# A residual chain of four conditioned layers on one core: V of four pairs in one burst of small tiles, a shorter setup, and a new order of each turn

## The chip, the cores and the metric

The kernel runs on one core of a Trainium2 chip. The time is device microseconds of one execution; the median of three executions of the kernel before is 199.01 us (198.2 to 202.66). In the profiles PE is TensorE's matmul, PEld its weight load, DVE VectorE, ACT ScalarE, POOL GpSimd, and SP the engine that here only issues transfers.

## The reference

The input x has 64 batches of 64 tokens of 512 features. Four layers follow each other, each a residual, and all are linear:

```
x = x + x Wb^T + scale0[e] * ((x Wt^T) A0[e]^T B0[e]^T) Wp^T     (e: one of 4)
x = x + x W1^T + scale1[f] * (x A1[f]^T) B1[f]^T                 (f: one of 8)
x = x + mix over the 64 token rows by w2[g]                      (g: one of 8)
x = x + mix over the 64 token rows by w3[h]                      (h: one of 200)
```

The last two work on the token axis, the first two on the feature axis, so they commute. The kernel makes one 512x512 matrix g01 of the two dense parts (with the identities), low-rank tables u and V (V has 16 rows per adapter, 64 + 128 in all) and, for each batch, one 64x64 token matrix p. Then out = (p x) g01 + ((p x) u) V.

## The kernel before, in words

Two batches make a pair (128 rows); four pairs make a turn; there are 8 turns. Turn 0 and turn 7 are written out, turns 1 to 6 are a hardware loop. No scheduler sets an order: each engine runs its own list as it is written, and semaphores hold the lists together.

PE's work of a turn, in the names of the code and of the profile:
- **reduce** (out z_ps): z = y u, for the two pairs of a half; 16 matmuls of 128 rows by 32 columns with 64 tokens. Float32 operands, which the profile lists as two instructions for each matmul (x32).
- **mix** (out y_ps): y = p x, in 64x64 tiles, four of them in different quarters of the array; 32 matmuls for two pairs, x64 in the profile.
- **token_mix** (out p_ps): the p of the next turn, 8 matmuls of 64x64, x16.
- **apply** (out o_ps): 12 matmuls of 128x128 by 512 columns for one pair, from yy (y split in a rounded high part and the rest, type fp32r) and g01 (split the same way); one instruction each. Behind them, in the kernel before, 2 matmuls of the same size that add z V, again with a high and a low part of V.

Around it: DVE copies y out of PSUM (`copy_y`, 2 of 4 per half), ACT makes the high part (`high_y`), DVE the low (`low_y`). ACT and DVE add and split z (`z_half`, `sum_z`, `low_z`). ACT copies o out of PSUM (`copy_out`) and doubles V (`double_v`). DVE prepares the operands of token_mix two turns ahead: `add_w3` (one instruction) and `place_w2` (eight small copies by register addresses). PE waits for both in `token_ready`, ahead of the reduce of the turn before that p is used in. POOL selects u (`place_u`) and gathers w3 for a later turn by four indirect DMAs. SP issues the loads of x, the stores, and for each pair four transfers of 16 rows out of the table of V (`fetch_v`).

The setup computes g01, u and V from the weights: transposes, products and splits, with PE at their head; `g01_step(k)` is 12 matmuls, `up_k` are the tables of u for pairs of adapters.

## Time and profile before

| | |
|---|---|
| median of 3 executions | 199.01 us |
| the profiled execution | 200.97 us |
| its span, first to last instruction | 199.1 us |
| PE busy | 177.4 us, 89% |
| DVE, ACT, POOL busy | 96.8, 94.2, 71.7 us |
| granted TensorE clock | full in all 40 slices (2.4 GHz) |

PE is the engine to follow: where it is idle, the trace names what ended the wait. The start of a z_ps burst marks a half turn, so the distance of every second z_ps start is the length of a turn. The time of a burst is best read from its start to the start of the next one, since the ends of matmuls are modelled and overlap the next.

### The profile page before, as it was taken

To read this page: it belongs to the slowest core of one execution; us is meant where nothing else is said; L and a number is where in the kernel's file an instruction comes from. 1 tells how busy PE (TensorE), PEld (TensorE's weight loads), DVE (VectorE), ACT (ScalarE), POOL (GpSimd) and SP (SyncE) were. 2 spreads that over 40 slices of the span, in tenths; PEclk is the share of its full clock that TensorE was granted. 3 is DMA by queue.
4 is the path that set the end of the run, shared out by engine and by line. 5 is a ranking of instruction groups with operands and counts; after the bars stand their busy time and mean duration, and the time that the engine had idled before them with its cause. 6 is when DMAs were issued, how large, how long until landed. Compare 5 with 4: busy or idle time off the path is not lost.

```text
span 199.1 us, 7261 instructions
## 1 busy us (share of the span) xinstructions
PE 177.4 (89%) x2304; PEld 140.1 (70%) x2304; DVE 96.8 (49%) x232; ACT 94.2 (47%) x183; POOL 71.7 (36%) x184
## 2 busy tenths in 40 slices
PE   6599898696889699999898989898898989999992
PEld 6377574575668487878686867777686868787781
DVE  1288588629653651746074527524650646154210
ACT  2365742126336645455463636354544545564521
POOL 2525787030653056306521741373056303113000
PEclk9999999999999999999999999999999999999999
DMA  3999412222372846375555737482847375443412
GB/s 80 394 357 289 155 46 87 53 66 72 84 262 71 266 151 198 87 245 164 179 168 173 248 84 229 119 259 78 256 121 229 99 232 169 151 162 82 180 72 89
DMA packets 19081, 32.39 MB, mean 163 GB/s; under 512 B 5878, under 2 KB 5878, under 8 KB 19062
## 3 DMA queue, kind: packets, MB, share of 16 engines
q1 hardware_dynamic: 17744, 31.11, 50.0%
q0 software_dynamic: 1024, 1.05, 1.8%
q8 instruction: 8, 0.13, 0.3%
q14 instruction: 11, 0.09, 0.1%
q10 hardware_dynamic: 294, 0.01, 0.1%
HBM read 22.98 MB, written 9.18 MB: 162 GB/s over the span
## 4 chain that ended last, share of the span: by engine, by line
PE 59%; issue 11%; DVE 9%; ACT 9%; DVEq 6%; DMA 2%; another core or an unknown queue 1%; POOL 0%; SPq 0%; ACTq 0%
PE o_ps L733 35%; PE y_ps L733 8%; PE z_ps L733 5%; DVE y_all L619 4%; PE spare_ps L733 4%; PE p_ps L733 3%; ACT yy L444 3%; DVEq L667 3%; DVEq L657 2%; DMA w_sb<-in_L_cond_W_dram 2%; DVE w_sel L667 2%; ACT z L477 1%; ACT v_sel L458 1%; PE y_ps L745 1%
## 5 line engine op out<-in xcount | busy, mean ns | idle before, releaser
L733 PE MATMUL o_ps<-g,yy 128*128 128x512 f32 x384 | 95.2, 396 | 0.0
L733 PEld LDWEIGHTS o_ps<-g,yy 128*128 128x128 f32 x384 | 70.8, 188 | 16.2
L340 POOL COPY u_sel<-u_tab 128x64 f32 x128 | 28.0, 242 | 89.8 <-PE z_ps L733 70.1
L330 POOL DMA_INDIRECT w_all<-in_L_cond_weights_dram,w_rows x32 | 31.7, 990 | 12.8 <-issue 9.7
L465 ACT ACTIVATE o_sb<-o_ps 128x512 f32<-128x512 f32 x32 | 19.2, 599 | 33.8 <-PE o_ps L733 32.4
L444 ACT ACTIVATE yy<-y_all 128x512 fp32r<-128x512 f32 x32 | 19.6, 635 | 25.4 <-DVE y_all L619 21.5
L633 DVE TENSOR_TENSOR z_sum<-z_ps,z_half 64x128 f32<-64x128 f32 x16 | 4.5, 282 | 50.4 <-ACT z_half L472 50.4
L626 DVE TENSOR_TENSOR yy<-y_all,yy 128x512 fp32r<-128x512 f32 x32 | 20.7, 690 | 2.9 <-ACT yy L444 1.9
L619 DVE COPY y_all<-y_ps 128x512 f32<-128x512 f32 x32 | 20.6, 686 | 0.5
L733 PE MATMUL o_ps<-v_sel,z 128*128 128x512 f32 x64 | 20.1, 394 | 0.0
L733 PE MATMUL z_ps<-y_all,u_sel 128*32 128x64 f32 x512 | 11.6, 222 | 9.4 <-DVE w_sel L667 5.1
L733 PEld LDWEIGHTS z_ps<-y_all,u_sel 128*32 128x32 f32 x512 | 8.4, 109 | 16.1 <-issue 16.1
L667 DVE COPY w_sel<-w2T 64x64 f32 x64 | 14.6, 229 | 9.7 <-issue 5.0
L733 PE MATMUL y_ps<-p_now,x_raw 64*64 64x64 f32 x1024 | 18.9, 221 | 0.3 <-issue 0.3
L458 ACT ACTIVATE v_sel<-v_sel 64x512 fp32r<-64x512 f32 x32 | 18.5, 624 | 0.4
L733 PEld LDWEIGHTS y_ps<-p_now,x_raw 64*64 64x64 f32 x1024 | 16.6, 134 | 2.1 <-issue 0.8
L641 DVE TENSOR_TENSOR z<-z_sum,z 32x128 fp32r<-32x128 f32 x32 | 9.2, 287 | 12.4 <-ACT z L477 11.9
L733 PEld LDWEIGHTS o_ps<-v_sel,z 128*128 128x128 f32 x64 | 12.0, 188 | 2.5
L477 ACT ACTIVATE z<-z_sum 32x128 fp32r<-32x128 f32 x32 | 9.9, 311 | 6.9 <-DVE z_sum L633 6.5
L472 ACT ACTIVATE z_half<-z_ps 64x128 f32<-64x128 f32 x16 | 4.4, 275 | 6.6 <-PE z_ps L733 6.4
L450 ACT ACTIVATE p_now<-p_ps 128x256 f32<-128x256 f32 x8 | 3.1, 386 | 7.5 <-PE p_ps L733 5.2
L733 PE MATMUL p_ps<-w_now,w_sel 64*64 64x64 f32 x128 | 5.2, 220 | 1.1 <-issue 1.1
(124 smaller groups left out, 139.8 us busy)
## 6 DMA issues: line engine op xcount, KB each, us to landing
x_raw<-in_x_dram SPq DMA_DIRECT2D x16, 512.0 KB
v_sel<-v_table SPq DMA_DIRECT2D x128, 64.0 KB, 2.1
out_dram<-o_sb SPq DMA_DIRECT2D x14, 512.0 KB, 3.1
w_sb<-in_L_cond_W_dram SPq DMA_DIRECT2D x4, 256.0 KB, 4.8
wb_sb<-in_L_cond_W_base_dram SPq DMA_DIRECT2D x4, 256.0 KB, 6.3
wp_sb<-in_L_cond_Wp_dram SPq DMA_DIRECT2D x2, 512.0 KB, 6.8
wt_sb<-in_L_cond_Wt_dram SPq DMA_DIRECT2D x1, 1024.0 KB
out_dram<-o_sb SPq DMA_DIRECT2D x4, 256.0 KB, 2.8
```

The lines of the kernel that those rows point to most:

```text
L330: pool.indirect_dma_start(out=w3_all[:, j, :], out_offset=None, in_=w3_flat, in_offset=bass.IndirectOffsetOnAxis(ap=w3_rows[:, j:j + 1], a ...
L340: nc.gpsimd.tensor_copy(u_sel[u % 2][:, :, b, RANK * part:RANK * part + RANK], u_tab[:, :, bass.ds(e, 1), :].rearrange("p k a r -> p k (a r)")
L444: nc.scalar.activation(yy[u][:, :, 0, :], y_all[u % 2][:, :, :], ACT.Copy).then_inc(yh_set, 1)
L458: nc.scalar.activation(v_sel[u][ZR:, 0, :], v_sel[u][0:ZR, 0, :].bitcast(F32), ACT.Copy).then_inc(v_twice, 1)
L465: nc.scalar.activation(o_sb[:, u, :], o_ps[u % 2][:, :], ACT.Copy).then_inc(o_set, 1)
L477: nc.scalar.activation(z[rows, :, toks], z_sum[rows, :, :], ACT.Copy).then_inc(zh_set, 1)
L619: nc.vector.tensor_copy(y_all[u % 2][:, :, :].rearrange("p k (b t) -> p b k t", b=2), y_of(u)).then_inc(yf_set, 1)
L626: nc.vector.tensor_tensor(yy[u][:, :, 1, :], y_all[u % 2][:, :, :], yy[u][:, :, 0, :].bitcast(F32), ALU.subtract).then_inc(yl_set, 1)
L633: nc.vector.tensor_tensor(z_sum[:, :, :], z_of(slice(0, ZR)), z_half[:, :, :], ALU.add).then_inc(z_summed, 1)
L641: nc.vector.tensor_tensor(z[ZR + ZR // 2 * b:ZR + ZR // 2 * (b + 1), :, toks], z_sum[rows, :, :], z[rows, :, toks].bitcast(F32), ALU.subtr ...
L667: nc.vector.tensor_copy(w2_sel[rows, u, :], w2T[rows, bass.ds(g, 1), :].rearrange("p a c -> p (a c)")).then_inc(w2_placed, 1)
L733: return nc.tensor.matmul(dst, lhsT, rhs, start=start, stop=stop)
```

## The change

1. **V in one burst.** z and V stay plain float32. z holds 32 rows for each pair, in four groups of partitions; `close` issues for the four pairs of the turn 8 matmuls of 32 rows by 64 columns with 512 columns to stream (16 instructions). Each of the eight has its own 32x64 part of the array, and each pair its own PSUM bank: o_ps has four banks now. `sum_z`, `low_z`, `z_half`, `double_v` and the split of V are gone; `copy_z` on ACT copies z.
2. **The order of a turn on PE.** reduce(0), token_mix, apply 0, mix(1), apply 1, reduce(1), apply 2, close, mix(0) of the next turn, apply 3. close opens the sum of pair 3 and closes those of pairs 0 to 2, so these are copied out behind it: 0 and 2 by ACT, 1 by DVE. Pair 3 is copied by DVE when apply 3 is done (`copy_last`).
3. **V is fetched by POOL**, with two indirect DMAs of 128 rows a turn in place of 16 transfers on SP. SP alternates loads and stores.
4. **DVE's order.** place_w2 for two turns ahead moves ahead of the copies; add_w3 moves to the end, behind copy_last.
5. **Setup.** v0 and u0T are computed in plain float32, as 4 + 4 matmuls in the two column halves, where there were 12 + 12 fp32r matmuls and the splits of wt, wpT, b0 and a0T. Four matmuls of g01_step(0) start before the low parts exist. token_mix(0) and mix(0) go ahead of g01 steps 2 and 3, and `copy_y` of turn 0 ahead of the low parts of g01. The ids and scales are loaded by SP and spread over 128 partitions, with `find_row_shift` and `find_v_rows` on DVE.

The core of the diff:

```diff
-            def apply(i, u):
-                n = u % 2
-                wait(pe, o_set, QUAD * i + u - 1)
-                pe.wait_ge(yl_set, QUAD * i + u + 1)
...
-                pe.wait_ge(zl_set, 2 * (2 * i + u // 2 + 1))
-                pe.wait_ge(v_twice, QUAD * i + u + 1)
-
-                mm(o_ps[n][:, :], z[:, n, :], v_sel[u][:, 0, :], False, False)
-                mm(o_ps[n][:, :], z[:, n, :], v_sel[u][:, 1, :], False, True).then_inc(o_done, 1)
+            def close():
+
+                for u in range(QUAD):
+                    opens = u == QUAD - 1
+                    for b in range(2):
+                        rows, to = z_rows(u, b), slice(SEQ * b, SEQ * b + SEQ)
+                        mm(o_ps[u][to, :], z[rows, u // 2, :], v_sel[rows, u // 2, :],
+                           opens, not opens).then_inc(v_done, 1)
...
+            def turn(i, first=False, last=False):
+                reduce_ready(i, 0)
+                if not first and not last:
                     token_ready(i + 1)
...
+                reduce(0)
+                if not first and not last:
+                    token_mix(i + 1)
+                apply(i, 0, lambda: mix_ready(i, 1), first)
+                mix(1)
+                apply(i, 1)
+                reduce_ready(i, 1)
...
+                reduce(1)
...
+                apply(i, 2, v_ready)
+                close()
+                if not last:
+                    mix(0)
+                apply(i, 3, behind_v=True)
```

```diff
+            def copy_last(i):
+                dve.wait_ge(o_done, QUAD * (i + 1))
+
+                wait(dve, o_out[1], 16 * i)
+                nc.vector.tensor_copy(o_sb[:, QUAD - 1, :], o_ps[QUAD - 1][:, :]).then_inc(o_set_dve, 1)
+
+            def turn(i, ahead=True, more=True):
+                pass_y(i, 1)
+                if ahead:
+                    place_w2(i + 2)
+                copy_out(i, 1)
                 if more:
...
+                    pass_y(i + 1, 0)
+                    copy_last(i)
+                if ahead:
                     add_w3(i + 2)
```

```diff
+            def fetch_v(i):
+
+                wait(pool, v_done, 2 * QUAD * i)
+                for h in range(2):
+                    pool.indirect_dma_start(
+                        out=v_sel[:, h, :], out_offset=None, in_=v_table,
+                        in_offset=bass.IndirectOffsetOnAxis(ap=v_rows[:, h, i:i + 1], axis=0)
+                    ).then_inc(v_in, 16)
```

```diff
             for s in range(KC):
-                pe.wait_ge(setup_dve, DVE_DONE[f"wpT_{s}"])
-                for a, b in ((0, 0), (0, 1), (1, 0)):
-                    last = mm(bank_of("v0")[0:R0, :], b0_by[:, a, s, :, :].rearrange("p e r -> p (e r)"),
-                              wpT[:, b, s, :], s == 0 and a == b == 0, s == KC - 1 and a == 1)
+                mm(bank_of("u0T")[0:R0, :], b0_now[:, s, :, :].rearrange("p e r -> p (e r)"), wpT[:, s, :],
+                   s == 0, s == KC - 1)
+                last = mm(bank_of("u0T")[R0:, :], a0T[:, s, :], wt_sb[:, s, :], s == 0, s == KC - 1)
...
-            product(bank_of("u0T")[0:R0, :], lambda a, k: a0T[:, a, k, :],
-                    lambda b, k: wt[:, b, k, :]).then_inc(setup_ps, 1)
```

PE, the first turn of the kernel before, from its first reduce to the second pair's V (names without buffer numbers; a row's `waits` are the semaphores that its engine waits for ahead of it):

```order
L733 MATMUL z_ps<-y_all,u_sel 32x64 [waits x_in1,u_placed,p_set,yf_set,setup_dve]
L733 MATMUL z_ps<-y_all,u_sel 32x64 x15
L733 MATMUL y_ps<-p_now,x_raw 64x64 x32
L733 MATMUL o_ps<-g,yy 128x512 [waits yl_set]
L733 MATMUL o_ps<-g,yy 128x512 x11
L733 MATMUL o_ps<-v_sel,z 128x512 [waits v_twice,zl_set]
L733 MATMUL o_ps<-v_sel,z 128x512
L733 MATMUL p_ps<-w_now,w_sel 64x64 [waits p_set,w3_plus,w2_placed]
L733 MATMUL p_ps<-w_now,w_sel 64x64 x7
```

PE, the second half of the same turn in the changed kernel:

```order
L726 MATMUL z_ps<-y_all,u_sel 32x64 [waits w2_placed,w3_plus,z_set,p_set,u_placed,yf_set]
L726 MATMUL z_ps<-y_all,u_sel 32x64 x15
L726 MATMUL p_ps<-w_now,w_sel 64x64 x8
L726 MATMUL o_ps<-g,yy 128x512 [waits yl_set]
L726 MATMUL o_ps<-g,yy 128x512 x10
L726 MATMUL o_ps<-g,yy 128x512 [waits x_in0,p_set,v_in,z_set]
L726 MATMUL o_ps<-v_sel,z 64x512 x8
L726 MATMUL y_ps<-p_now,x_raw 64x64 x32
L726 MATMUL o_ps<-g,yy 128x512 [waits yl_set]
L726 MATMUL o_ps<-g,yy 128x512 x11
```

The two V matmuls behind each pair's twelve have become eight narrow ones, once a turn, ahead of the next mix and of pair 3's twelve.

DVE, the end of the loop's turn in the kernel before, from the last low part of y to the copies of place_w2:

```order
L626 TENSOR_TENSOR yy<-y_all,yy 128x4x128 [waits o_done,yh_set] x2
L650 REGISTER_ALU
L35 ISA [waits w3_in2]
L653 ISA [waits p_done]
L653 TENSOR_TENSOR w_now<-w_all,ident 128x256
L657 REGISTER_ALU [waits p_done]
L657 TENSOR_LOAD g_code
L657 ISA x2
L667 REGISTER_ALU
L667 ISA
L667 COPY w_sel<-w2T 64x64
```

DVE, the end of the loop's turn in the changed kernel, behind its place_w2:

```order
L659 COPY o_sb<-o_ps 128x512 [waits o_out0]
L614 ISA
L35 REGISTER_ALU [waits y_done]
L35 REGISTER_ALU [waits z_done]
L618 COPY y_all<-y_ps 128x2x4x64 [waits yl_set]
L618 COPY y_all<-y_ps 128x2x4x64 [waits yl_set,z_done,y_done]
L622 REGISTER_ALU
L625 TENSOR_TENSOR yy<-y_all,yy 128x4x128 [waits o_done,yh_set] x2
L671 COPY o_sb<-o_ps 128x512 [waits o_out1,o_done]
L634 REGISTER_ALU
L637 ISA [waits p_done,w3_in2]
L637 TENSOR_TENSOR w_now<-w_all,ident 128x256
```

The copy that waits for o_done of pair 3 (L671) stands ahead of w_now (L637); PE's next turn in the loop waits for that w_now (w3_plus) ahead of its first reduce.

## Rows read from the trace of the kernel before

**Rows 1.** Page: busy us, share, instructions; granted clock in tenths in 40 slices.
```profile
PE 177.4 (89%) x2304; PEld 140.1 (70%) x2304; DVE 96.8 (49%) x232; ACT 94.2 (47%) x183; POOL 71.7 (36%) x184
...
PEclk9999999999999999999999999999999999999999
```

**Rows 2.** Waits of PE, 69 to 171 us: total us, times, longest.
```profile
PE z_ps L733 <- DVE w_sel L667: 5.1, 6, 1.6
PE z_ps L733 <- issue: 2.2, 4, 0.6
```

**Rows 3.** Timeline of PE in a loop turn: start, us, group, [idle before].
```profile
106.59 0.65 PE L733 MATMUL z_ps<-y_all,u_sel 128*32 128x64 f32 x32 [0.81 <-DVE w_sel L667]
...
116.57 0.22 PE L733 MATMUL z_ps<-y_all,u_sel 128*32 128x64 f32 x1 [0.58 <-issue]
...
125.33 0.65 PE L733 MATMUL z_ps<-y_all,u_sel 128*32 128x64 f32 x32 [0.82 <-DVE w_sel L667]
```

**Rows 4.** Timeline of PE, turn 6 and the start of turn 7.
```profile
162.83 0.65 PE L733 MATMUL z_ps<-y_all,u_sel 128*32 128x64 f32 x32 [0.79 <-DVE w_sel L667]
163.41 1.16 PE L733 MATMUL y_ps<-p_now,x_raw 64*64 64x64 f32 x64
164.39 0.65 PE L733 MATMUL p_ps<-w_now,w_sel 64*64 64x64 f32 x16
164.97 3.06 PE L733 MATMUL o_ps<-g,yy 128*128 128x512 f32 x12
...
171.07 0.63 PE L733 MATMUL o_ps<-v_sel,z 128*128 128x512 f32 x2
171.63 0.65 PE L733 MATMUL z_ps<-y_all,u_sel 128*32 128x64 f32 x32
172.22 1.16 PE L733 MATMUL y_ps<-p_now,x_raw 64*64 64x64 f32 x64
173.31 3.03 PE L733 MATMUL o_ps<-g,yy 128*128 128x512 f32 x12
176.18 0.63 PE L733 MATMUL o_ps<-v_sel,z 128*128 128x512 f32 x2
176.64 2.91 PE L733 MATMUL o_ps<-g,yy 128*128 128x512 f32 x12
179.39 0.63 PE L733 MATMUL o_ps<-v_sel,z 128*128 128x512 f32 x2
179.94 0.65 PE L733 MATMUL z_ps<-y_all,u_sel 128*32 128x64 f32 x32
```

**Rows 5.** Timeline of DVE at the end of a loop turn.
```profile
100.37 1.29 DVE L619 COPY y_all<-y_ps 128x512 f32<-128x512 f32 x2
...
102.97 0.42 DVE L653 TENSOR_TENSOR w_now<-w_all,ident 128x256 f32<-128x256 f32 x1
104.26 2.20 DVE L667 COPY w_sel<-w2T 64x64 f32 x8 [0.87 <-issue]
```

**Rows 6.** Busy us of each engine in stretches of three loop turns (x: instructions).
```profile
115.85:116.50 0.65, 0.15 (x11) 0.00 (x0) 0.00 (x0) 0.00 (x0) 0.00 (x0) 1.00 0.50 139
```

**Rows 7.** Timeline of POOL in a loop turn.
```profile
114.68 0.95 POOL L330 DMA_INDIRECT w_all<-in_L_cond_weights_dram,w_rows  x1 [0.31 <-issue]
```

**Rows 8.** Chain that ended last, setup: start us, us, what.
```profile
16.00 0.47 PE y_ps L782 x4
...
19.73 2.97 PE spare_ps L733 x12
...
31.38 2.81 PE p_ps L733 x12
...
36.28 0.63 PE y_ps L745 x4
```

**Rows 9.** Timeline of DVE in the setup.
```profile
20.74 1.39 DVE L541 TENSOR_TENSOR w2T<-p_ps,ident 64x512 f32<-64x512 f32 x2
22.16 0.42 DVE L541 TENSOR_TENSOR a0T<-y_ps,a0T 128x256 fp32r<-128x256 f32 x1
24.55 0.69 DVE L541 TENSOR_TENSOR v0T<-y_ps,v0T 128x512 fp32r<-128x512 f32 x1 [1.97 <-ACT v0T L393]
```

**Rows 10.** Timeline of PE around turn 0.
```profile
45.99 1.16 PE L733 MATMUL y_ps<-p_now,x_raw 64*64 64x64 f32 x64
48.71 0.65 PE L733 MATMUL z_ps<-y_all,u_sel 128*32 128x64 f32 x32 [1.56 <-issue]
...
69.63 0.58 PE L733 MATMUL z_ps<-y_all,u_sel 128*32 128x64 f32 x26 [1.58 <-DVE w_sel L667]
```

**Rows 11.** Chain that ended last, its end.
```profile
195.61 0.60 ACT o_sb L465
```

More of the change, by code:

```diff
@@ L508, in _ @@
+            act.wait_ge(o_out[1], 16 * (QUADS - 1))
+            nc.scalar.activation(o_sb[:, QUAD - 1, :], o_ps[QUAD - 1][:, :], ACT.Copy).then_inc(o_set, 1)
         @block.vector
@@ L905, in half, with reduce @@
-                done.then_inc(z_done, 1)
-                if more:
-                    mix(part)
-                if h == 0 and not first and not last:
-                    token_mix(i + 1)
-                apply(i, 2 * h)
-                if h == 0 and first:
+                wait(pe, z_set, 2 * i + h)
+            def reduce(h):
+                for k in range(KC):
+                    for u in range(2 * h, 2 * h + 2):
+                        for b in range(2):
+                            done = mm(z_ps[z_rows(u, b), 0:SEQ], u_sel[u % 2][:, k, b, :],
+                                      y_all[u % 2][:, k, SEQ * b:SEQ * b + SEQ], k == 0, k == KC - 1)
+                done.then_inc(z_done, 1)
```

409 lines of the change are left out of this document (193 added, 216 removed), and 6 rows, old and new, of the table ORDER.

## The prediction, made before the changed kernel ran

> **What bounds the kernel now.** The page's first part says where to look: PE is busy 89% of the span, no other engine half of it [rows 1]. PE's waits come next. In the loop it waits 5.1 us for the last copy of place_w2 and some 2.2 us for "issue" [rows 2]. The timeline of a loop turn shows where: 0.8 us ahead of its first z_ps, and 0.6 us inside the second [rows 3]. The turn lasts from 106.59 to 125.33, 18.74 us. Turn 6, behind which no place_w2 stands, lasts from 162.83 to 179.94, 17.11 us, with no wait inside [rows 4]: that is PE's own work, and a turn between pays 1.6 us of waits on top. So the change can gain in three places: PE's work, the waits, and the setup, which holds turn 0 back until 48.71 [rows 10]. The clock is at its upper level, 2.4 GHz, all through [rows 1] and gives nothing.
>
> **PE's work of a turn, before.** From start to start [rows 4]: reduce 0.59 (171.63 to 172.22), mix 1.09 (172.22 to 173.31), token_mix 0.58 (164.39 to 164.97). Twelve o_ps matmuls that follow a burst of small tiles take 2.87 (173.31 to 176.18), twelve that follow their like 2.75 (176.64 to 179.39); two V matmuls 0.46 in the middle and 0.55 ahead of a small-tile burst. So entering an o stretch costs 0.12 and leaving it 0.09, and a stretch of twelve alone between bursts costs 2.87 + 0.09 = 2.96.
>
> **PE's work of a turn, after.** The turn has the same 48 o matmuls, in four stretches and not two: 4 x 2.96 = 11.84. Two reduces 1.18, two mixes 2.18, token_mix 0.58 together 3.94. New is the V burst, which no row shows. A float32 matmul is two instructions; 128-column float32 instructions take 0.47 for four, 0.118 each (at 16.00, [rows 8]), so 512 columns take 0.47 and a V matmul 0.94 by itself. Side by side the trace shows four tiles: 64 y_ps instructions take 1.09, 0.017 each, though four at a time are 0.068 apart [rows 4]. The bounds: if the float32 passes of 512 columns ran like an fp32r matmul (2.75 / 12 = 0.23) and all eight side by side, 0.46; if none ran beside another, 16 x 0.47 = 7.5. I take eight abreast, since each has rows, columns and a bank of its own as the four of y_ps have: 0.94, and 0.06 for issuing and leaving, 1.0. Sum: 11.84 + 3.94 + 1.0 = 16.8 us, against 17.11. The V matmuls save 64 x 0.23 = 14.7 us in the whole kernel, of which the burst takes back 8.0 and the two more stretches per turn 3.4: PE's work hardly falls, 0.3 a turn.
>
> The Trainium skill (TensorE: Matmul & The Clock Gate, Measured speedup vs the span model) gives 3.07x for four row tiles and 10.6x for sixteen tiles, so packing pays less than the number of tiles. By a factor of some 5.5 for eight, an estimate from that page, the burst would be 8 x 0.94 / 5.5 = 1.4 us and the sum of the kernel 3 us higher; four tiles of y_ps in this trace show no such loss.
>
> **The waits.** The wait for place_w2 goes: it now runs behind the copies of pairs 2 and 3, early in the turn. Its 2.20 us of copies with 0.87 ahead [rows 5] fall under apply 1, reduce(1) and apply 2, 6.5 us. If that cover were gone, its 3.1 us would stand ahead of copy_out of pair 1, whose late end delays the next y. What is late next is add_w3. It stands behind copy_last, which waits for the end of apply 3, PE's last work of the turn, and PE's next reduce waits for add_w3. So in the changed kernel PE must stand still once a turn: an o matmul ends 0.07 after the start that the next z_ps would have (171.70 against 171.63, rows 4), the semaphore some 0.05, copy_last until the next instruction can start 0.6 (two such copies take 1.29 [rows 5]), w_now 0.42, and 0.12 from DVE's end to PE's start (106.47, where eight copies that start at 104.26 end after 2.20, to 106.59 [rows 3, 5]). Together 1.3 us, ahead of turns 1 to 6. Turns 0 and 7 need none. What is queued behind: reduce(0), token_mix, apply 0. On DVE nothing is, since the next y comes 5 us later. This stall is larger than the 0.8 that it replaces.
>
> The other wait, 0.6 to 0.7 us inside the second reduce, is no wait of PE alone: between 115.85 and 116.50 no engine starts anything, PE only drains 11 matmuls [rows 6]. It follows the end of the turn's last indirect DMA (114.68 + 0.95 = 115.63, 9.0 us into the turn from 106.59 [rows 3, 7]). Turn 6 gathers nothing and has no such pause. The gather keeps its place after the first reduce, so the pause comes 9.1 us into the turn again, where the changed PE has begun apply 2. There twelve matmuls of 0.23 stand queued and cover it. I cost it at nothing; without the cover it is 0.7 in each of six turns.
>
> POOL's two V fetches cost 2 x (0.95 + 0.31) = 2.5 us of its time [rows 7], behind the V burst of the turn before. V is needed 14 us later, and POOL's turn, some 13 us with place_u and the gather, fits in 18. SP loses 16 transfers a turn and waits for nothing that PE needs. The z work leaves DVE and ACT and was hidden; two PSUM copies move from ACT to DVE, one of them the copy_last above.
>
> **Setup.** (a) g01_step(0) starts some 0.7 earlier, but the a0 flip still waits for its transfer, so the first product does not profit. (b) That product needs a0T from DVE, which stands behind w2T. Two passes of 0.6 fewer stand ahead, so a0T is ready at 22.6 - 1.0 = 21.6, and the product runs 4 x 0.94 = 3.8 with its pairs abreast, to some 25.4; before, v0 ended at 22.7 [rows 8, 9]: 2.7 later. (c) The next five products stay the same, 8.7 us (22.70 to 31.38), to 34.1. (d) The u0T product and the wait behind it, 31.38 to 36.28 [rows 8], are gone. The gu1 flip stands at 34.1, 2.2 earlier. (e) From that flip to the end of mix(0), 36.28 to 47.1, PE has the same work in another order. Before, 1.6 us of waiting followed, since copy_y stood behind the low parts of g01 [rows 10]; now copy_y is done under g01_step(3). Turn 0 starts at 34.1 + 10.8 = 44.9 to 45.0, 3.7 us earlier. Bounds: 2.7 more if the a0T chain costs nothing, nothing gained at all if the ids and b1, which are loaded later, come late.
>
> **The sum**, against the span 199.06 of the profiled execution. Setup -3.7. Turn 0: 20.92 before (48.71 to 69.63); after 16.8 + 0.2 for the low parts of g01 + 1.3 = 18.3: -2.6. Turns 1 to 5: 93.2 before (69.63 to 162.83); after 5 x 18.1 = 90.4: -2.8. Turn 6: 17.1 to 16.8: -0.3. Turn 7: 15.67 before (179.94 to 195.61 [rows 11]); after 0.59 + 4 x 2.96 + 1.09 + 0.59 + 1.0 + 0.1 = 15.2: -0.5. The end is the same, one copy and one store. Together -10, a span of 189.0. The span of before is 199.06 and the median 199.01 (the profiled execution took 200.97), so I forecast a median of 189.0 us.
>
> **The rivals.**
> - *The pause moves to the chain behind apply 3.* The fetch of V is also two indirect DMAs, and ends some 3 us after the V burst, while DVE works up to copy_last. If it brings a 0.7 us pause there, the stall grows to 2.0: 6 x 0.7 more, 193.2. For: the gather of every loop turn has one. Against: one gather in the setup shows none that PE feels.
> - *Turn 0 does not start earlier*: 189.0 + 3.7 = 192.7. For: more transfers ahead of b1 and of x, ten chained small DVE instructions. Against: DVE waits 2.0 us for v0T there [rows 9].
> - *The V burst runs four abreast*, as many as the trace shows: 0.94 more in each of 8 turns, 196.5, within 2%.
> - *The V burst runs one after another or nearly so*, since the tiles of 32 rows share the columns of their half: up to 7.5 - 1.0 = 6.5 more per turn, 189 + 52 = 241, slower. It decides from a burst of 2.8 us on, three times its size in the forecast, (203.0 - 189.0) / 8 = 1.75 more per turn. Against: two row tiles of y_ps share columns and run together [rows 4].
> - *The change does not make the stall*: if w_now is ready in time, 6 x 1.3 less, 181.2. Only an order other than the one built would do that.
>
> **How the numbers follow.** Forecast 0.55 (187 to 191), pause moved 0.14, no earlier start 0.09, four abreast 0.12, serial 0.05, no stall 0.05. About 2% is what a measurement can tell: below 195.0 is faster, above 203.0 slower. Faster: 0.55 + 0.14 + 0.09 + 0.05 less a little for two of them together, 0.81; the same 0.13; slower 0.06. The range takes the forecast with its bounds below (the a0T chain free: 186.3), the next two and the burst of four tiles: 186 to 196.5. It leaves out serial and no stall.
>
> **What would show each step.** The o_ps<-v_sel,z group: 128 instructions, eight bursts of 1.0 us from start to start. z_ps waits ahead of turns 1 to 6 for DVE w_now (L637), 1.2 to 1.3 idle each, and the chain goes over o_sb L671. No wait for w_sel. No idle inside apply 2. The first z_ps of turn 0 at 45, turns of 18.1, turn 6 of 16.8. I am wrong if the V burst is over 1.5, if the turns are over 18.8, or if turn 0 starts behind 47.

## The result and the profile after

The changed kernel took **238.6 us** in the median of four runs (236.1 to 246.1) beside 199.7 for the kernel before (198.2 to 202.7), which ran in the same job on the same chip: 1.194 of it, interval 1.176 to 1.211. The forecast was 189.0, with a range up to 196.5. It was wrong in sign and by 50 us.

One fact has to be told ahead of everything else, since no number can be read without it. Each job here ran a few kernels and the kernel before on one chip, and **the kernel before itself has two times**: 199.7, 200.9 and 200.1 us in three jobs (here called the 200 condition), 193.2, 192.7 and 192.7 in three others (the 193 condition). Two jobs on one chip found one condition each, so it isn't a property of the chip; what sets it was not found. The changed kernel was run in four jobs: 1.194, 1.190 and 1.196 in the 200 condition, and **1.014 (1.006 to 1.023), 194.7 us**, in the 193 condition. The prediction was made from a trace of the 200 condition. That 194.7 lies inside the forecast's range (186 to 196.5) is luck: in that condition the kernel before takes 192.7, so the change is 1.4% slower there and not 5% faster. All ratios are to the kernel before of the same job.

The ratios use only executions near the fastest of their kernel, so they differ a little from the quotients of the medians, and the execution profiled first (246.1 us, span 244.4; the others have spans of 234 to 238) is not in its ratio, though its loop turns show the same pauses as the later profiles of this kernel.

Page of the changed kernel, first part and granted clock, against [rows 1]:

```profile
span 244.4 us, 6445 instructions
...
PE 200.2 (82%) x2360; PEld 143.4 (59%) x2360; DVE 89.0 (36%) x211; ACT 50.2 (21%) x98; POOL 78.6 (32%) x194
...
PEclk9995699998899999997979799779979799899999
```

PE is busy longer (200.2 us, 177.4 before) though its work shrank, and its share fell: the clock drops in twelve of forty slices, which it did in none before. The view of waits, PE (total us, times, longest), against [rows 2]:

```profile
PE y_ps L726 <- issue: 12.4, 31, 1.1
PE z_ps L726 <- DVE w_now L637: 10.7, 6, 1.9
PE z_ps L726 <- DVE y_all L618: 6.0, 2, 3.0
```

The w_sel wait is gone. The w_now stall stands ahead of six turns, as forecast, but is 1.8 us long on average and not 1.3. The other two lines were in no forecast: 12.4 us of pauses *inside* the y bursts, and waits of up to 3.0 us for a copy of y. One loop turn (the second) in the timeline (start us, us, engine and group, [idle before]), against [rows 3]:

```profile
97.46 0.65 PE L726 MATMUL z_ps<-y_all,u_sel 128*32 128x64 f32 x32 [1.69 <-DVE w_now L637]
...
101.62 1.51 PE L726 MATMUL y_ps<-p_now,x_raw 64*64 64x64 f32 x61
102.23 0.97 POOL L314 DMA_INDIRECT w_all<-in_L_cond_weights_dram,w_rows  x1 [0.45 <-issue]
...
103.55 0.33 PE L726 MATMUL y_ps<-p_now,x_raw 64*64 64x64 f32 x3 [0.41 <-issue]
103.81 3.02 PE L726 MATMUL o_ps<-g,yy 128*128 128x512 f32 x12
...
106.00 0.94 POOL L314 DMA_INDIRECT w_all<-in_L_cond_weights_dram,w_rows  x1 [0.30 <-issue]
...
108.29 1.29 DVE L618 COPY y_all<-y_ps 128x512 f32<-128x512 f32 x2 [11.07 <-remote]
109.81 0.65 PE L726 MATMUL z_ps<-y_all,u_sel 128*32 128x64 f32 x32 [2.98 <-DVE y_all L618]
...
110.64 4.62 PE L726 MATMUL o_ps<-g,yy 128*128 128x512 f32 x12 [0.17 <-DVE yy L625]
115.18 1.11 PE L726 MATMUL o_ps<-v_sel,z 32*64 32x512 f32 x16
116.22 1.03 PE L726 MATMUL y_ps<-p_now,x_raw 64*64 64x64 f32 x52
116.82 0.97 POOL L323 DMA_INDIRECT v_sel<-v_table,v_rows  x1 [3.30 <-PE o_ps L726]
...
118.18 0.35 PE L726 MATMUL y_ps<-p_now,x_raw 64*64 64x64 f32 x4 [0.41 <-issue]
...
119.19 3.04 PE L726 MATMUL o_ps<-g,yy 128*128 128x512 f32 x12
```

The V burst at 115.18 is done 1.04 us later, as forecast. The y bursts beside it aren't: 2.19 us (101.62 to 103.81) and 2.97 (116.22 to 119.19), where the same 64 records take 1.09 in [rows 4]. Both lie under POOL's indirect DMAs. The copies of y, whose last matmul was recorded before 103.9, begin only at 108.29, 1.3 us behind the end of the last gather (106.94); PE stands still for it for 3.0 us, and then runs apply 2 in 4.5 us and not 3.

The same stretches of a turn in the 193 condition, from the profile of the unedited changed kernel there (e20, below):

```profile
102.15 0.65 PE L726 MATMUL z_ps<-y_all,u_sel 128*32 128x64 f32 x32 [1.40 <-DVE w_now L637]
...
106.29 1.16 PE L726 MATMUL y_ps<-p_now,x_raw 64*64 64x64 f32 x64
107.09 0.97 POOL L314 DMA_INDIRECT w_all<-in_L_cond_weights_dram,w_rows  x1 [0.45 <-issue]
...
107.99 1.29 DVE L618 COPY y_all<-y_ps 128x512 f32<-128x512 f32 x2 [6.07 <-PE y_ps L726]
...
114.90 1.24 PE L726 MATMUL y_ps<-p_now,x_raw 64*64 64x64 f32 x64
...
115.50 0.98 POOL L323 DMA_INDIRECT v_sel<-v_table,v_rows  x1 [1.05 <-PE o_ps L726]
...
120.49 0.65 PE L726 MATMUL z_ps<-y_all,u_sel 128*32 128x64 f32 x32 [1.40 <-DVE w_now L637]
```

Here the DMAs lie beside the bursts and no pause is listed; the burst beside the fetches of V takes 1.18 and not 1.09, the one beside the gathers 1.10. Where one turn's 8.25 us went, stretch by stretch (the two timelines above, from the start of each stretch to the start of the next):

| stretch of PE's turn | 200 condition | 193 condition | more |
|---|---|---|---|
| z, p, apply 0 | 4.16 | 4.14 | 0.02 |
| y, second half, under the gathers | 2.19 | 1.10 | 1.09 |
| apply 1, until the second z | 6.00 | 2.94 | 3.06 |
| z and apply 2 | 5.37 | 3.53 | 1.84 |
| V burst | 1.04 | 1.04 | 0 |
| next y, first half, under the fetches of V | 2.97 | 1.18 | 1.79 |
| apply 3 and the wait for w_now | 4.86 | 4.41 | 0.45 |
| sum | 26.59 | 18.34 | 8.25 |

Of the 1.84 of z and apply 2, 1.6 is the clock and 0.2 a wait for DVE's yy. The windows of the two stretches (length, busy us of PE, PEld, DVE, ACT, POOL with instructions, granted clock, DMA share, GB/s), first in the 200 condition:

```profile
109.81:115.18 5.37, 5.20 (x45) 3.81 (x45) 2.89 (x10) 0.73 (x2) 1.73 (x8) 0.68 0.24 89
```

and in the 193 condition:

```profile
110.33:113.86 3.53, 3.53 (x45) 2.67 (x45) 2.40 (x10) 0.23 (x1) 2.38 (x8) 1.00 0.25 89
```

The same 45 matmuls ran at a mean clock of 0.68 behind 3 us of idle, and at 1.00 without it. But idle time of that length doesn't always bring the clock down: in the turn before, the same wait of 2.98 us stands ahead of 84.86, and the clock stayed:

```profile
84.86:88.59 3.73, 3.59 (x44) 2.67 (x44) 2.81 (x10) 0.70 (x2) 1.43 (x7) 1.00 0.34 118
```

The table is one turn, and only the first two turns of the loop lose their time in this way. In turns 3 to 5 the y burst under the gathers itself takes 3.6, 4.9 and 3.9 us, no wait for a copy of y follows, and applies of 12 matmuls run at the lower clock (1.2 GHz) ahead of it and behind it. Turn 4:

```profile
152.20 4.49 PE L726 MATMUL o_ps<-g,yy 128*128 128x512 f32 x12
...
161.39 0.21 PE L726 MATMUL y_ps<-p_now,x_raw 64*64 64x64 f32 x1 [1.08 <-issue]
```

In both forms the copies of y start 1.3 to 1.5 us behind the end of the last gather. The five turns are 24.9 to 27.6 us long.

Turn lengths, first z_ps to first z_ps (the changed kernel has two more profiles in the 200 condition, e7 and e16, with means of 26.1 and 25.3 for turns 1 to 5):

| kernel, condition | turn 0 starts | turn 0 | mean of turns 1 to 5 | turn 6 |
|---|---|---|---|---|
| before, 200 (first profile) | 48.71 | 20.92 | 18.64 | 17.11 |
| before, 200 (e8) | 51.70 | 20.52 | 18.14 | 17.09 |
| before without gathers, 193 (e21) | 48.42 | 18.57 | 17.09 | 17.09 |
| forecast of after | 45.0 | 18.3 | 18.1 | 16.8 |
| after, 200 | 48.91 | 23.62 | 26.66 | 20.23 |
| after, 193 (e20) | 47.15 | 18.28 | 18.36 | 16.87 |
| no gathers, 193 (e1) | 46.74 | 18.24 | 18.36 | 16.86 |
| no gathers, 200 (e18) | 47.55 | 20.27 | 20.49 | 18.61 |
| V by SP, 193 (e14) | 46.80 | 19.40 | 19.89 | 18.17 |
| V by SP, 200 (e19) | 47.49 | 21.99 | 25.15 | 18.09 |
| transfers moved, w3 early, 193 (e12) | 48.26 | 16.80 | 16.80 | 16.80 |
| transfers moved, w3 early, 200 (e17) | 46.41 | 16.80 | 16.80 | 16.80 |

### The profile page after: what moved, and what is told of

Same layout as the page of the kernel before. It is cut to its first block and busy times, and to the rows that moved or that the text cites. A ratio compares the mean times of both kernels' runs of the same rounds, so it can differ in the third digit from the quotient of the medians.

```text
span 244.4 us, 6445 instructions
## 1 busy us (share of the span) xinstructions
PE 200.2 (82%) x2360; PEld 143.4 (59%) x2360; DVE 89.0 (36%) x211; ACT 50.2 (21%) x98; POOL 78.6 (32%) x194
## 5 line engine op out<-in xcount | busy, mean ns | idle before, releaser
L726 PE MATMUL o_ps<-g,yy 128*128 128x512 f32 x384 | 110.4, 441 | 1.7 <-issue 1.4
L726 PEld LDWEIGHTS o_ps<-g,yy 128*128 128x128 f32 x384 | 78.7, 213 | 24.9 <-issue 5.4
L726 PE MATMUL y_ps<-p_now,x_raw 64*64 64x64 f32 x1024 | 29.5, 224 | 13.3 <-issue 12.4
L323 POOL DMA_INDIRECT v_sel<-v_table,v_rows x16 | 15.3, 959 | 16.5 <-PE o_ps L726 13.2
L441 ACT ACTIVATE o_sb<-o_ps 128x512 f32<-128x512 f32 x16 | 8.7, 594 | 35.5 <-PE o_ps L726 35.5
L659 DVE COPY o_sb<-o_ps 128x512 f32<-128x512 f32 x8 | 5.5, 692 | 26.9 <-PE o_ps L726 26.9
L726 PE MATMUL o_ps<-g,wb 128*128 128x512 f32 x48 | 11.8, 398 | 0.9 <-ACT wb L387 0.9
L726 PEld LDWEIGHTS o_ps<-g,wb 128*128 128x128 f32 x48 | 8.8, 188 | 3.0 <-ACT wb L387 1.1
L726 PE MATMUL o_ps<-v_sel,z 32*64 32x512 f32 x128 | 8.9, 613 | 0.0
L726 PE MATMUL z_ps<-wpT,b_now 128*64 128x512 f32 x8 | 6.5, 995 | 2.1 <-DVE a0T L571 2.1
```

The lines of the kernel that those rows point to most:

```text
L323: pool.indirect_dma_start(out=v_sel[:, h, :], out_offset=None, in_=v_table, in_offset=bass.IndirectOffsetOnAxis(ap=v_rows[:, h, i:i + 1], ...
L441: nc.scalar.activation(o_sb[:, u, :], o_ps[u][:, :], ACT.Copy).then_inc(o_set, 1)
L659: nc.vector.tensor_copy(o_sb[:, u, :], o_ps[u][:, :]).then_inc(o_set_dve, 1)
L726: return nc.tensor.matmul(dst, lhsT, rhs, start=start, stop=stop)
```

## The experiments

Four explanations were on the table. Theory A: POOL's indirect DMAs hold the other engines up where they lie beside PE's bursts of short matmuls, and the clock falls in the idle that follows. Rivals as they came: the new order itself is too tight (B), all is one of the chip's condition (C), or it takes both kinds of indirect DMA together (D).

### First job (before took 193.2): taking the transfers away

The edits of this and the later jobs are to the changed kernel, if nothing else is said.

**e1**, no gathers in the turns (and no wait of DVE for them).

```diff
-                    if h == 0 and i < QUADS - 2:
-                        pool.wait_ge(w3_plus, i + 2)
-                        gather_w3(range(QUAD * (i + 2), QUAD * (i + 3)))
```

> The changed kernel without POOL's w3 gathers in the turns; it leaves out the w3 of pairs 8 and up and uses that of pairs 4 to 7 in their place. Theory A (while POOL issues indirect DMAs, and for about 1 us behind them, no engine's sequencer gets on; it costs where PE runs short instructions or waits for a copy, and the idle time then costs clock): turns 1 to 5 come from 26.6 us to the 20.2 of turn 6, which has no gather, mix(1) to 1.09, and no wait of 3.0 us ahead of the second z_ps: about 205 us. Theory B (the order itself is too tight: copy_y of pairs 2, 3 has only apply 1 to hide under, the idle time lets the clock fall): the order is the same, so 235 to 240 us.

Measured: 194.8 us, 1.016 (1.006 to 1.026): below what either theory gave.

**e2**, V through 16 small transfers a turn by SP, half of them ahead of store(i, 0) and half behind it, in place of POOL's two.

```diff
-                        if h == 0 and i > 0:
-                            fetch_v(i)
...
+                    if h == 0:
+                        fetch_v(i + 1, range(0, 2))
                     store(i, h)
+                    if h == 0:
+                        fetch_v(i + 1, range(2, 4))
```

> The changed kernel with V fetched as before, by 16 transfers of SP a turn, and not by POOL's two indirect DMAs; the gather stays. Theory A: mix(0) comes from 2.97 to 1.09 us in seven turns, and DVE's chain to w_now is some 0.6 us shorter; mix(1) and the wait ahead of the second z_ps stay: about 222 us. Theory B: 235 to 240 us. Theory C (SP's small transfers were what kept V off the critical path badly, more of them hurt): over 240.

Measured: 208.1, 1.084 (1.072 to 1.097), again below all that was expected. PE waits 7.2 us for loads of x.

**e3**, both edits.

> Both edits at once: no indirect DMA in any turn (the w3 of pairs 8 and up is left out, that of pairs 4 to 7 used). Theory A: turns of 16.8 + 1.3 us as forecast, V burst of 1.05, setup as measured (turn 0 starts at 48.9): 193 us, clock full. Theory B: 235 to 240 us, the clock still falls.

Measured: 205.5, 1.073 (1.061 to 1.084). A miss: slower than e1, which keeps two indirect DMAs a turn. Its waits show why; SP's 16 issues, some 0.7 us each (eight in 5.5 us), stand ahead of the loads of x:

```profile
PE z_ps L730 <- DVE w_now L641: 7.8, 6, 1.3
PE o_ps L730 <- DMA x_raw<-in_x_dram: 6.8, 6, 1.4
```

**e4**, the kernel before without its gathers (the same lines).

> The kernel before without its w3 gathers in the turns (w3 of pairs 8 and up left out, that of pairs 4 to 7 used). Theory A: the pause of 0.6 to 0.7 us inside the second z_ps of turns 1 to 5 and the delay in turn 0 go, place_w2 ends as much earlier: 194 to 196 us. Theory B says nothing of it; if the pause belongs to PE's own instruction supply or to SP's transfers, it stays and the time is 199.

Measured: 191.7, 0.994 (0.989 to 1.000). A small gain; by the pause in the trace of before it should have been 3 to 5 us.

What followed at that point was a wrong reading: that leaving the gathers out takes the loss away, 1.194 to 1.016. It compared two jobs. e2 kept the gathers, and its y bursts beside them take 1.10 to 1.27 us; e1 kept the fetches of V, and its bursts take 1.16 to 1.18: in this job an indirect DMA cost a burst 0.2 us at most.

### Second job (before took 200.9): the control

**e7**, the changed kernel unedited.

> The changed kernel without any edit, on the same chip as the other experiments. The first four experiments were compared with a kernel before that took 193.2 us, while the changed kernel was compared with one that took 199.7. In them, V through SP (gathers kept) and the gathers left out (V by POOL kept) each took nearly the whole loss away, though they take away different transfers, and the mixes beside the transfers that were left ran at their usual 1.1 us. Theory A, the two kinds of POOL transfer together hold up the other engines: the loss is there again, ratio 1.17 to 1.21, about 230 us beside 193, loop turns of 25 to 28 us. Theory C, the hold-up was of that chip or of that time, and a POOL transfer costs the engines nothing here: turns of 18.4 us as where the gathers were left out, ratio 1.00 to 1.03, 194 to 199 us.

Measured: 237.6, 1.190 (1.174 to 1.206): the loss is back on the chip on which e1 to e4 ran. **e8**, the kernel before unedited, for a profile beside it.

> The kernel before without any edit, for a profile of it on this chip. Theory A: the pause of 0.66 us after the last gather (116.5 us in the first profile) and loop turns of 18.7 us on average are there, span 190 to 192 only because other stretches are shorter. Theory C: no pause after the gather, loop turns near 17.4 us as in the run that left the gathers out, and a span 7 to 9 us under the 199.1 of the first profile.

Measured: 200.7, 1.004 (0.997 to 1.011), span 199.1. Neither expectation holds whole: the pause is there, loop turns are 18.1. In turns 2 to 5 the pause stands in the second z burst, which begins under the last gather, as in [rows 6]; in turn 1 of both profiles of before it stands in the y burst behind it (1.72 and 1.74 us). So the trace of before had met a y burst once. From e8's timeline:

```profile
98.65 0.95 POOL L330 DMA_INDIRECT w_all<-in_L_cond_weights_dram,w_rows  x1 [0.30 <-issue]
...
99.33 0.65 PE L733 MATMUL z_ps<-y_all,u_sel 128*32 128x64 f32 x31
100.51 0.22 PE L733 MATMUL z_ps<-y_all,u_sel 128*32 128x64 f32 x1 [0.53 <-issue]
```

**e9**, no gathers in the turns, and add_w3 early.

```diff
             def turn(i, ahead=True, more=True):
                 pass_y(i, 1)
                 if ahead:
                     place_w2(i + 2)
+                    add_w3(i + 2)
                 copy_out(i, 1)
                 if more:
                     pass_y(i + 1, 0)
                     copy_last(i)
-                if ahead:
-                    add_w3(i + 2)
```

> The changed kernel without the gathers in the turns, and with add_w3 of a turn ahead of the copies of o on DVE (before: behind copy_last, the last of the turn). Leaves out: pairs 8 and up use the w3 of pairs 4 to 7. The wait of PE for w_now at a turn's start was 1.3 to 1.4 us, 6 times, without the gathers (8.3 us in all, turns of 18.36 us; 16.86 in the one turn without it). If it is DVE's order alone, turns 0 to 5 shrink to 16.9 us and the span from 191.9 to 183.6, ratio about 0.975 where it was 1.016. Rival: behind w_now another copy (the y of the next turn's first half) is just as late, and PE waits for that: less than 3 us gained, ratio over 1.00.

Measured: 198.6, 0.994 (0.988 to 1.000). By its time this fits neither expectation. The w_now wait is gone from the view of waits; turns are 18.67 and not 16.9. The difference is 1.8 in the y burst (2.95 us) beside the fetches of V, which e1 did not have:

```profile
115.48 1.52 PE L722 MATMUL y_ps<-p_now,x_raw 64*64 64x64 f32 x56
117.41 0.35 PE L722 MATMUL y_ps<-p_now,x_raw 64*64 64x64 f32 x4 [0.41 <-issue]
```

**e10**, w3 of turns 2 and up loaded by SP (8 plain transfers at the start of a turn), add_w3 early; computes everything.

```diff
+            def fetch_w3(i):
+                for u in range(QUAD):
+                    code = sp.value_load(w3_code[0:1, bass.ds(QUAD * i + u, 1)], min_val=0, max_val=255 * 257)
+                    for b in range(2):
+                        e = nc.s_assert_within((code >> (8 * b)) & 255, 0, 199)
+                        sp.dma_start(w3_all[SEQ * b:SEQ * b + SEQ, bass.ds(QUAD * i + u, 1), :]
+                                     .rearrange("p a c -> p (a c)"),
+                                     w3_flat[bass.ds(e * SEQ, SEQ), :]).then_inc(w3_in[2], 16)
```

> The changed kernel with the w3 of turns 2 and up loaded by SP as plain transfers (8 per turn at the turn's start, two blocks of 64x64 per pair, their rows from a code in a register) and not gathered by POOL, and add_w3 ahead of the copies of o. Computes all of it. Theory A (POOL's two kinds of indirect transfer together are the cost): turns of 16.9 us, span 184 to 185, ratio 0.97 to 0.98. Rival: SP's 8 transfers of some 0.65 us push its loads of x back, as 16 did for V (6.8 us of waits for x in all): turns of 17.5 to 18 us, ratio 1.00 to 1.02.

Measured: 205.1, 1.030 (1.020 to 1.040), above both expectations and by neither's reason. No wait for x is listed. The y burst beside the fetches takes 3.45 us, and in three of the turns the clock falls in the apply behind it (a mean of 0.62 in the one shown), which it does not in e9:

```profile
119.24:122.69 3.45, 2.08 (x72) 1.73 (x65) 1.03 (x2) 1.08 (x2) 1.91 (x2) 0.98 0.54 186
122.69:127.04 4.35, 4.35 (x12) 3.15 (x11) 2.58 (x4) 1.23 (x2) 0.00 (x0) 0.62 0.92 333
```

The burst took 2.95 in e9, and the other 0.5 us of it isn't explained.

### Third job (before took 192.7): moving the transfers

**e13**, e1 again; **e14**, e2 again.

> The changed kernel without the gathers in the turns, a second time (leaves out: pairs 8 and up use the w3 of pairs 4 to 7). The kernel before took 193.2 us when this was first run and 200.9 when the changed kernel was run again, so the two belong to two conditions of the chip, and this run is for the second one. If the kernel before takes about 200 now: theory A, both kinds of POOL transfer hold PE up in that condition, each where it falls on a burst of short matmuls: the pause of 1.8 us in the y burst beside fetch_v stays, w_now is waited for besides, turns of 20.2 us as turn 6 of the changed kernel has, span 203 to 206, ratio 1.02 to 1.04. Theory D, only the two kinds together: turns of 18.4, ratio 0.97 to 0.99.

> The changed kernel with V loaded by SP in 16 transfers a turn, gathers by POOL kept, a second time. In a condition where the kernel before takes 200: theory A, the gathers alone cost what the trace of the changed kernel shows around them: 1.1 us in the y burst, 3.0 us of idle before the second z, and applies at half clock behind it, some 5 us in each of turns 0 to 5; with SP's waits for x 225 to 235 us, ratio 1.12 to 1.17. Theory D, only the two kinds together: 1.04 to 1.08 as the first time.

Measured: 194.2, 1.012 (1.001 to 1.022), and 206.0, 1.075 (1.063 to 1.087). This job, on another chip, came out in the 193 condition, so these say only that the first job's numbers stand.

**e11**, the same six indirect DMAs a turn, each begun behind a burst of short matmuls, so that it runs beside long ones. Computes everything.

```diff
                         if h == 0 and i > 0:
+                            pool.wait_ge(y_done, QUAD * i + 2)
                             fetch_v(i)
                         pool.wait_ge(z_done, 2 * i + h + 1)
+                        if h == 1 and i < QUADS - 2:
+                            gather_w3(range(QUAD * (i + 2) + 2, QUAD * (i + 3)))
...
                         pool.wait_ge(w3_plus, i + 2)
-                        gather_w3(range(QUAD * (i + 2), QUAD * (i + 3)))
+                        pool.wait_ge(y_done, QUAD * i + 4)
+                        gather_w3(range(QUAD * (i + 2), QUAD * (i + 2) + 2))
```

> The changed kernel with the same transfers by POOL, but issued under bursts of long matmuls: fetch_v waits for the end of the next y's first half (so it runs under apply 3), two of the four gathers for the end of y's second half (under apply 1), the other two for the second z (under apply 2). Computes all of it. Theory A with the place as the cost (short matmuls are held up, long ones are not): the y bursts take 1.1 us again and the idle before the second z goes, turns of 18.1 to 18.6 us, span 192 to 196, ratio 0.97 to 1.00. Rival, any POOL transfer holds up the semaphores of the others wherever it is issued: the copies behind y and z come late as before, turns of 22 us and more, ratio over 1.08.

Measured: 193.7, 1.007 (1.003 to 1.012). In this condition there is next to nothing for the move to save (turns of 18.21 us in the mean where e20 has 18.36), so it doesn't test the theory, and e11 was not run in the other condition.

**e12**, e11 with add_w3 early.

> The same, with add_w3 ahead of the copies of o on DVE. Computes all of it. If the place is the cost and the wait for w_now is DVE's order alone: 1.3 us less in each of six turns than without, turns of 16.9 to 17.2, span 184 to 188, ratio 0.93 to 0.95. If the w3 of the late two gathers isn't there yet when DVE comes to it (it lands some 2 us behind its issue): DVE waits and the copies of o behind it are late, no gain.

Measured: **185.6, 0.963 (0.953 to 0.972)**, with turns of 16.80 us; the ratio is a little above the expected 0.93 to 0.95. Against e11 it is 8.1 us, and e11's wait for w_now adds up to 7.9 in six times: the stall was DVE's order alone.

### Fourth job (before took 200.1): each kind of transfer alone, and the move

**e16**, unedited; **e17**, e12 again; **e18**, e1 again; **e19**, e2 again.

> The changed kernel without any edit, for the other condition of the chip. If before takes 193 us in this job: theory C, a POOL transfer costs the engines nothing in this condition, turns of 18.4 us and a ratio of 1.01 to 1.03; theory D, the two kinds of transfer together, a ratio of 1.17 to 1.21. If before takes 200 again: 1.19 as twice before, and the three other kernels decide.

> The kernel with POOL's transfers under long matmuls and add_w3 early, a second time. Where before takes 193: 0.96 again. Where before takes 200: if the place of the transfers is the cost, the loop's turns stay at 16.8 to 17.3 us, 185 to 190 us, ratio 0.93 to 0.95; if any transfer of POOL holds the others up there, turns of 20 us and more, ratio over 1.02.

> The changed kernel without the gathers in the turns, a third time (leaves out: pairs 8 and up use the w3 of pairs 4 to 7). Where before takes 193: 1.01 again. Where before takes 200: the fetches alone cost 1.8 us a turn (theory A), turns of 20.2, 205 us, ratio 1.02 to 1.03.

> The changed kernel with V loaded by SP in 16 transfers a turn and the gathers by POOL kept, a third time. Where before takes 193: 1.08 again. Where before takes 200: theory A, the gathers alone cost some 5 us in each of six turns, ratio 1.12 to 1.17; theory D 1.04 to 1.08.

| | ratio here (before 200) | ratio in the 193 condition | more |
|---|---|---|---|
| e16, both kinds by POOL | 1.196 (1.179 to 1.214) | 1.014 (e20) | 0.18 |
| e18, fetches of V alone | 1.056 (1.044 to 1.069) | 1.016, 1.012 | 0.04 |
| e19, gathers alone | 1.199 (1.185 to 1.213) | 1.084, 1.075 | 0.12 |
| e17, both, moved, w3 early | **0.935 (0.924 to 0.946)** | 0.963 (e12) | -0.03 |

Each kind costs alone, 0.04 and 0.12, so D falls and A stands, in this condition. The two don't simply add: e19's 1.08 in the other condition is waits for x (7.2 us in e2), and of these only 1.0 us is listed in e19, so 0.12 understates the gathers. By the length of a turn, they cost 6.8 us (25.15 for 18.36) and the fetches 2.1 (20.49), and both together 6.9 to 8.3. The ratios of e18 and e19 are above what theory A gave them (1.02 to 1.03, 1.12 to 1.17): the kind of the loss is as expected, its size was too low. The gathers cost more because they hold the burst, then the copies behind it. e18's burst under the two fetches:

```profile
101.08 1.52 PE L722 MATMUL y_ps<-p_now,x_raw 64*64 64x64 f32 x56
101.67 0.97 POOL L323 DMA_INDIRECT v_sel<-v_table,v_rows  x1 [1.44 <-PE o_ps L722]
...
102.96 0.36 PE L722 MATMUL y_ps<-p_now,x_raw 64*64 64x64 f32 x4 [0.37 <-issue]
103.99 3.03 PE L722 MATMUL o_ps<-g,yy 128*128 128x512 f32 x12
```

and e19's under the four gathers, 6.0 us for 64 records, with the apply behind it at the lower clock:

```profile
99.34 0.91 PE L734 MATMUL y_ps<-p_now,x_raw 64*64 64x64 f32 x45
99.35 0.97 POOL L336 DMA_INDIRECT w_all<-in_L_cond_weights_dram,w_rows  x1 [0.46 <-issue]
...
103.60 0.27 PE L734 MATMUL y_ps<-p_now,x_raw 64*64 64x64 f32 x2 [0.45 <-issue]
105.01 0.41 PE L734 MATMUL y_ps<-p_now,x_raw 64*64 64x64 f32 x7 [1.14 <-issue]
105.35 4.55 PE L734 MATMUL o_ps<-g,yy 128*128 128x512 f32 x12
```

The last group comes 0.95 us behind the end of the last gather (104.06), and the other y burst of the turn (114.43 to 115.52), which no DMA lies beside, takes 1.09.

e17 keeps all six and pays nothing. Its timeline, the DMAs beside the o matmuls, the copies of y on time in the middle of them:

```profile
100.96 1.16 PE L730 MATMUL y_ps<-p_now,x_raw 64*64 64x64 f32 x64
102.05 3.02 PE L730 MATMUL o_ps<-g,yy 128*128 128x512 f32 x12
...
102.38 1.29 DVE L622 COPY y_all<-y_ps 128x512 f32<-128x512 f32 x2 [4.77 <-PE y_ps L730]
102.93 0.97 POOL L314 DMA_INDIRECT w_all<-in_L_cond_weights_dram,w_rows  x1 [1.44 <-PE y_ps L730]
...
106.13 0.94 POOL L314 DMA_INDIRECT w_all<-in_L_cond_weights_dram,w_rows  x1 [0.64 <-PE z_ps L730]
```

and its window of one turn, PE busy 16.80 of 16.80 us:

```profile
96.81:113.61 16.80, 16.80 (x273) 12.51 (x272) 8.72 (x20) 4.36 (x9) 9.23 (x22) 1.00 0.50 168
```

It takes 184.5 us where the kernel before takes 200.1 and 185.6 where it takes 192.7: the condition no longer reaches it. This version beats the kernel before in both.

Two limits. e17 differs from e16 by two edits, the move and w3 early. What w3 early is worth by itself in this condition is seen only without gathers and across jobs, some 10 us (e18 to e9) of the 52. The move shows in its y bursts, which take 1.09 us again though all six DMAs are there. And not every short burst beside such a DMA is held: in each gathering loop turn of e17 the second z burst (105.00 here) begins 0.5 us before the record of the second gather ends (105.49), and takes its usual 0.58 us. In the held y bursts, too, the first 43 to 61 of the 64 records mostly go at the usual rate, and only the rest come in handfuls. This could be PE's supply of instructions running out; no run tested that.

### Fifth job (before took 192.7): the missing corner

**e20**, the changed kernel unedited; **e21**, e4 again.

> The changed kernel without any edit. Where before takes 193 us: the fetches alone and the gathers alone cost PE nothing in its y bursts there, so turns of 18.4 us, 194 to 198 us, ratio 1.01 to 1.03. Where before takes 200: 1.19 a fourth time.

> The kernel before without the gathers in its turns (leaves out: pairs 8 and up use the w3 of pairs 4 to 7). Where before takes 193: 0.994 again. Where before takes 200: if the gathers are what makes before 7 us slower there, this takes 192 to 194 us in both conditions, ratio 0.96 to 0.97; if something else does, it takes 198 to 200, ratio over 0.99.

Measured: 194.7, 1.014 (1.006 to 1.023), and 192.2, 0.999 (0.994 to 1.003). B falls, since the same order has turns of 18.36 us here. C is right: in this condition the fetches cost a y burst 0.1 us (1.18 for 1.09) and the gathers nothing that can be measured, and in the kernel before e4 and e21 leave 0 to 1% for the gathers. Whether before's gathers are the whole of its 7 us between the conditions was not run where it could be seen.

## Why the prediction was wrong

**The V burst: right.** Forecast 1.0 us eight abreast, measured 1.04 to 1.05 from start to start in every turn, in every profile looked at; the one exception is a turn of e2 in which the granted clock was 0.50, with 1.94. The four-abreast and serial rivals are out. The estimate of 1.4 us worked out from the Trainium skill (TensorE: Matmul & The Clock Gate, Measured speedup vs the span model) was not borne out: the measured burst is 0.10 us above the 0.94 that the prediction gave a single V matmul. That 0.94 was itself a little high: the float32 instructions of the u0T product, 512 columns and two abreast, come 0.43 us apart at full clock (e20), which is 0.86 for a matmul and a factor of 6.6 for eight, where the estimate took 5.5.

**PE's work of a turn: right.** Forecast 16.8 us; e12 and e17, which have no waits left in the turns, take 16.80 in every turn from 0 to 6, and turn 6 of e20 16.87. Turn 7, forecast 15.2, is 15.2 in the first profile (226.07 to 241.25, the last copy of o).

**The stall for w_now: right in kind and nearly in size.** Forecast 1.3 ahead of turns 1 to 6; measured 1.4 (8.3 us in six) in the 193 condition, with turns of 18.36 for 18.1. It came from reading DVE's order against PE's. The two handovers were sized too small: the 0.05 for the semaphore stood in no row, and in e20 copy_last starts 0.15 us behind the modelled end of apply 3 (119.24 against 119.09), and z_ps 0.24 and not 0.12 behind w_now (120.49 against 120.25). That the change pays 8 us for it and gets them back from one swap on DVE (e12 against e11) the prediction could have said and didn't: its rival "no stall" was priced right at 8 us but dismissed as another order.

**The pause behind the gather: this is the step that failed.** This holds for the 200 condition, in which the prediction was made and first measured. The text costed it "at nothing", since it would come "9.1 us into the turn again, where the changed PE has begun apply 2" and twelve queued matmuls cover it. Three things were wrong with it.
- It took the pause to be something that comes once, at the gather's end. The runs show that in the 200 condition a burst of 64 short matmul records beside indirect DMAs gets through some 50 of them and is then issued a few at a time (mostly two to six) with some 0.4 us between, for as long as the DMAs go on. Before, only the tail of the gather met a short burst, so the trace showed 0.58 of it ([rows 3] and [rows 6]).
- It took the place from the end of the gather and not from its start. In the changed kernel the gather began 0.6 us into the y burst (102.23 against 101.62), and in e19 with it. In the turn of the table it cost 1.1 us in the burst, 3.1 waiting for the copies behind it and 1.8 in apply 2, mostly clock, 6.0 us in all; priced at 0, at 0.7 without cover. In turns 3 to 5 it was 2.5 to 3.8 in the burst and the rest in applies at the lower clock.
- The cover counted was PE's queue alone. The copies of y on DVE, for which PE waits next, came late too (1.3 to 1.5 us behind the end of the last gather), and nothing covers them.

**The fetches of V: failed in size.** Costed at nothing for PE, with a rival of 0.7 us a turn in "the chain behind apply 3" at 0.14. They begin 0.6 us into the next y burst and cost 1.8 there, and 0.45 more ahead of the next z, since the copies of y, copy_last and w_now all end later. The place that the rival named was wrong: it is the burst, not the chain behind it.

**The two together, and the clock.** The clock was said to give nothing, since it stood at 2.4 GHz all through [rows 1]. It fell in many turns once PE stood idle or was held: 4.5 us from start to start for twelve matmuls that take 2.95. Where it falls behind a wait of 3.0 us it adds 1.6. It did not fall in every such turn (84.86, above), and no term of the sum stood for it.

**The gain that was forecast on the waits was the condition's.** Turns 1 to 5 were to shrink from 18.64. In the 193 condition the kernel before has hardly such turns to give. That is inferred, since the unedited kernel was not profiled there: the two without gathers, which equal it in time within 1%, have 17.09 (e21) and 17.34 (e4), with 0 and 1.0 us of the wait for w_sel that was 5.1 [rows 2], and without the pause. So the change there takes on 8.3 us of stall, and gets back 1.3 us of setup (48.42 to 47.15), 1.7 in turn 0, 0.2 in each later turn and half a microsecond at the end: 1.4% slower, and not 5% faster.

**Setup: forecast 3.7 us earlier, got from 0.2 later to 2.3 earlier.** Turn 0 starts at 48.9 in the first profile and between 46.4 and 48.7 in the others; the forecast was 45.0, and before it was 48.71. Steps (c) to (e) hold: from the end of the first product to turn 0 it takes 19.1 us in the first profile (29.8 to 48.9), forecast 19.5. Step (b) failed: a0T was to be ready at 21.6 (two passes of 0.6 are 1.2 and not the 1.0 taken off, which makes it 21.4) and the product to take 3.8. It was ready at 23.0. The windows of the first profile, and the product's start:

```profile
20.00:24.00 4.00, 1.89 (x9) 0.85 (x9) 2.40 (x4) 0.00 (x0) 3.09 (x4) 0.50 0.73 261
24.00:26.00 2.00, 2.00 (x8) 0.73 (x6) 0.00 (x0) 0.00 (x0) 1.50 (x2) 0.50 0.34 114
...
23.21 1.09 PE L726 MATMUL z_ps<-wpT,b_now 128*64 128x512 f32 x1 [2.12 <-DVE a0T L571]
```

PE waited 2.5 us for w2's transfer and 2.1 for a0T, the granted clock was 0.50, and the product took 6.5 us (23.21 to 29.8). An earlier place for a step whose input comes no earlier is idle time, and here the clock was at its lower level for most of what came next.

**The chances.** The range took each unknown by the nearest row. A rival with POOL's transfers beside y bursts, at the pause's own rate, was not among them: the trace had the pause in each loop turn that gathers, in turn 1 in a y burst, and it was explained away rather than placed.

## What to carry to other kernels

Before moving work, lay the start *and* end of every software-issued (indirect) DMA against the other engines' bursts, before and after the move; a pause that a trace shows at one edge of an overlap can run through all of it when the overlap grows. Begin such DMAs behind a semaphore that puts them beside long instructions: two waits and a later place for two of the gathers, together with w3 early, took 22% off this kernel's time in one condition (e16 to e17), and the move by itself cost nothing in the other (e11). Look at every turn of a loop and not at one: the same cause showed as a wait for a copy in some turns and as a longer burst in others. And run the unedited kernel beside the edits before comparing across jobs: the first four experiments looked like an answer and were a change of condition.

## What the hardware showed beyond what was expected

- The condition itself: one unchanged kernel takes 192.7 to 193.2 us in some jobs and 199.7 to 200.9 in others. It shows in what POOL's indirect DMAs do to PE: the DMAs themselves mostly take the same 0.94 to 0.98 us in both. What is held (the supply of instructions, their issue, the semaphores) and what sets the condition stays open. In the first profile a y burst recorded as done by 103.9 let the copies start at 108.3, so there more than the matmuls was late; in e19 the matmuls themselves were. In the first profile, e7, e9, e16, e18 and e19 the copies of y behind a held burst start 0.8 to 1.8 us behind the end of the last indirect DMA.
- PE's clock fell to its lower level behind a wait of 2.98 us in one turn of the first profile and not in the turn before, behind the same wait. It fell after waits of 2.5 us (first profile) and 2.8 us (e20) in the setup. It did not fall behind the held bursts of e18 and e9, which have gaps of 0.4 us and take 2.8 to 3.0 us in all; in e10, with 0.5 us more in that burst, it fell in three turns of five. So idle time of one length gave both outcomes here.
- Eight float32 matmuls of 32 rows by 64 columns, which are sixteen instructions, take 1.04 us for 512 columns each, 0.065 us per instruction, against 0.25 for one 128-row matmul of the same columns in fp32r (2.95 / 12).
